# Products that nobody reads on TensorE ahead of six places where it waits, in a fused audio-tower kernel

## The reference

```python
h = _L0_tok_ref(x, ...)                       # merges 16 frames to 8 by a small softmax attention
h = h + _L0_attn_ref(_layernorm(h), ...)      # a Mamba block: input projection, causal convolution, scan, output projection
h = h + _L0_ffn_ref(_layernorm(h), ...)       # 8 experts, each token goes to its best two
h = h + _L1_attn_ref(_layernorm(h), ...)      # linear attention with decay: (q k^T / sqrt(d) * M) v
h = h + _L1_ffn_ref(_layernorm(h), ...)       # 3 experts, each sequence of 32 tokens goes to its best one
```

## Time and profile before

| | |
|---|---|
| median of 3 runs | 624.76 us (622.01 to 624.86) |
| the profiled execution, its own time | 630.95 us |
| its span, first to last instruction | 628.8 us |
| mean granted TensorE clock in the span | 0.899 |
| busy: PE / PEld / DVE / ACT / POOL | 520.4 / 452.6 / 359.6 / 242.8 / 222.8 us |

### The profile page before, as it was taken

One profiled execution on the slowest core, in us unless ns is written; L12 is line 12 of the kernel. 1 busy time (PEld: TensorE's weight loads), 2 busy tenths in 40 slices (PEclk: granted clock), 3 DMA queues, 4 the chain that ended last, 5 costly groups with the idle time before them and its releaser, 6 DMA issues. The chain is left out here.

```text
span 628.8 us, 11806 instructions
## 1 busy us (share of the span) xinstructions
PE 520.4 (83%) x3467; PEld 452.6 (72%) x3467; DVE 359.6 (57%) x1116; ACT 242.8 (39%) x579; POOL 222.8 (35%) x332
## 2 busy tenths in 40 slices
PE   4999879959989612999999999997687842999995
PEld 3667768847877502899999999995576741889994
DVE  2466538887999796444545454442456643445543
ACT  1368756664675250222222222222535541222230
POOL 1144500004977420212121221203777313466541
PEclk9999859988999755999999999997579985899998
DMA  9992000005232260131131311111335321122210
GB/s 263 244 205 50 2 0 2 0 2 145 83 104 71 73 276 7 39 95 39 53 87 47 92 45 45 40 37 40 88 88 158 99 78 33 49 65 63 64 52 19
DMA packets 39766, 47.84 MB, mean 76 GB/s; under 512 B 5633, under 2 KB 33618, under 8 KB 39586
## 3 DMA queue, kind: packets, MB, share of 16 engines
q1 hardware_dynamic: 32754, 33.48, 19.1%
q0 software_dynamic: 6000, 12.30, 7.2%
q10 hardware_dynamic: 960, 1.38, 0.8%
HBM read 31.56 MB, written 10.32 MB: 67 GB/s over the span
## 5 line engine op out<-in xcount | busy, mean ns | idle before, releaser
L1469 ACT ACTIVATE hidden_room<-psum 128x768 f32<-128x768 f32 x57 | 46.2, 811 | 206.6 <-PE psum L1429 193.7
L1380 POOL DMA_INDIRECT rows_in<-x,token x57 | 56.2, 986 | 176.3 <-PE psum L1407 155.3
L1513 DVE TENSOR_TENSOR rows_turned<-psum,rows_turned 128x128 fp32r<-128x128 f32 x57 | 16.6, 292 | 122.4 <-ACT rows_turned L1462 93.8
L1451 PE MATMUL psum<-w_proj,hidden_room 128*128 x468 | 82.6, 326 | 1.1 <-DVE hidden_room L1504 1.1
L1451 PEld LDWEIGHTS psum<-w_proj,hidden_room 128*128 128x128 f32 x468 | 75.1, 190 | 1.4 <-issue 1.3
L1429 PE MATMUL psum<-w_fc_high,rows_turned 128*128 x234 | 64.1, 356 | 8.1 <-DVE w_fc_low L1476 8.0
L1504 DVE COPY hidden_room<-psum 128x512 f32<-128x512 f32 x114 | 58.4, 552 | 3.5 <-PE psum L1438 0.9
L1438 PE MATMUL psum<-const,hidden_room 128*128 128x128 f32 x342 | 47.7, 276 | 0.9 <-ACT hidden_room L1469 0.9
L705 PE MATMUL psum<-w_fc_high 97*128 (+3 forms) x192 | 47.9, 413 | 0.6 <-PEq L401 0.6
L1429 PEld LDWEIGHTS psum<-w_fc_high,rows_turned 128*128 128x128 f32 x234 | 39.3, 192 | 12.3 <-issue 8.7
L788 DVE SCALAR_TENSOR_TENSOR conv_out<-psum,param,conv_out 128x496 f32<-128x496 f32 (+2 forms) x60 | 41.6, 715 | 8.0 <-ACT conv_out L727 6.6
(11 more groups left out here) (279 smaller groups left out, 1112.1 us busy)
## 6 DMA issues: line engine op xcount, KB each, us to landing
xbc_tile<-xbc SPq DMA_DIRECT2D x16, 320.0 KB, 2.8
w_proj<-in_w_proj SPq DMA_DIRECT2D x1, 4608.0 KB, 14.5
y<-rows_out SPq DMA_DIRECT2D x39, 96.0 KB, 1.6
sz<-in_x SPq DMA_DIRECT2D x16, 192.0 KB, 7.3
w_fc_low<-in_w_fc SPq DMA_DIRECT2D x2, 1536.0 KB, 30.8
w_fc_low<-in_w_fc SPq DMA_DIRECT2D x1, 2304.0 KB, 17.6
w<-in_w SPq DMA_DIRECT2D x3, 576.0 KB
x<-xf_tile SPq DMA_DIRECT2D x16, 96.0 KB, 1.6
```

Source lines behind the costliest of these rows:

```text
L1380: nc.gpsimd.indirect_dma_start(out=x[:, t.odd, 0:D], out_offset=None, in_=src, in_offset=bass.IndirectOffsetOnAxis(ap=tile_token[:, t.i:t. ...
L1451: last = nc.tensor.matmul(ps_y, ht[:, t.odd, ch, :], w_down[:, bass.ds((e * HC + ch) * D, D)], start=ch == 0, stop=ch == HC - 1)
L1469: act.activation(hid[:, t.odd, :], ps_h[t.odd], gelu).then_inc(act_done, 1)
L1513: nc.vector.tensor_tensor(xt[:, t.odd, REST, :], ps_x[:, 0, :], xt[:, t.odd, FIRST, :], ALU.subtract).then_inc(x_low, 1)
```

## The change

It adds a helper `stay_busy`, which issues a number of float32 products of a 128x128 tile with itself, and calls it at these places on PE: 9 products at the very start of the kernel (on a new tile that DVE sets to ones first), 6 ahead of the wait for the first frames, 4, 4 and 2 ahead of the first three `score`s; 28 after the last product of the projection; 7 when half and 7 when three quarters of the experts' low weights are ready, both ahead of `up(0)` of the first experts; 6 ahead of each of the first four `turn`s of the linear attention, after a new wait for `h3`; 4 after the last product of the sequence dispatch, 7 ahead of the loop over tiles of the second experts, and 3 ahead of their `up(0)`. That is 105 products. They write to a part of PSUM that nobody reads then; nothing waits for them but PE itself, whose queue is in order. Nothing is removed.

```diff
+def stay_busy(nc, to, of, count):
+
+    for _ in range(count):
+        nc.tensor.matmul(to, of, of, start=True, stop=True)
...
             @block.tensor
             def _(pe):
+                pe.wait_ge(square_set, 1)
+                stay_busy(nc, ps_none, square[:, :], 9)
                 pe.wait_ge(early, 16)
                 pe.wait_ge(w_ready, 3)
                 nc.tensor.transpose(ps_wv, wv_sel[:, :], c["ident"]).then_inc(wv_mm, 1)
 
                 def project(t):
+                    if t.i == 0:
+                        stay_busy(nc, ps_none, square[:, :], 6)
                     pe.wait_ge(x_in[t.i], 16)
...
                 def score(t):
+                    if t.i < 3:
+                        stay_busy(nc, ps_none, square[:, :], (4, 4, 2)[t.i])
                     pe.wait_ge(qk_ev, t.i + 1)
...
             @block.vector
             def _(dve):
+                nc.vector.memset(square[:, :], 1.0).then_inc(square_set, 1)
                 dve.wait_ge(early, 16)
...
                 with pe.Fori(1, N_TOK // SB) as j:
                     superblock(j)
+                pe.wait_ge(taps, 3 * (5 * (N_TOK // SB - 1) + 1))
+                stay_busy(nc, banks[0][:, 0:P], m.c["ident"], 28)
...
         nc.tensor.matmul(banks[3][:, 0:3 * T2], in_group[:, :], in_tile[:, :, :].rearrange("p w t -> p (w t)"), start=True, stop=True).then_inc(spread_mm, 1)
+        stay_busy(nc, banks[4][:, 0:P], m.c["ident"], 4)
...
         pe.wait_ge(routed.experts_set, 1)
+        if merge:
+            stay_busy(nc, ps_t[0][:, 0:P], c["ident"], 7)
...
         def up(t):
             if split and isinstance(t.i, int) and t.i == 0:
+                for done in (n_exp // 2, n_exp * 3 // 4):
+                    pe.wait_ge(split.low_ready, done)
+                    stay_busy(nc, ps_t[0][:, 0:P], c["ident"], 7)
                 pe.wait_ge(split.low_ready, n_exp)
             e = taken[t.i]
+            if merge and t.i == 0:
+                stay_busy(nc, ps_t[0][:, 0:P], c["ident"], 3)
             pe.wait_ge(x_out, x_outs * (t.i + 1))
...
                 def turn(t):
+                    if t.i < 4:
+                        pe.wait_ge(h3, t.i + 1)
+                        stay_busy(nc, ps[:, 7, 0:P], c["ident"], 6)
                     pe.wait_ge(std_set, t.i + 1)
```

More of the change, by code:

```diff
@@ L352, in merge_frames @@
         w_qk = sb("w_qk", [P, 2, G])
+        square = sb("square_that_nobody_reads", [P, P])
+        square_set = sem("square_set")
+        ps_none = banks[7][:, 0:P]
         wq_sc = sb("wq_scaled", [P, G])
```

## The result

The changed kernel takes 614.28 us (median of 4 runs, 613.46 to 617.17), the kernel before 624.81 us in the runs beside them (4 runs, 622.01 to 625.58). The ratio is 0.9845, with an interval of 0.9807 to 0.9883, so the kernel is faster by 1.2 to 1.9%. The ratios in this document leave out executions that lie over 1.5% above the fastest of their kernel, which is one reason why they differ from the quotients of the medians. The prediction was 609.0 us, in a range of 604.5 to 619.5: right in sign, inside the range, and right in the mechanism of four of its five terms, but 5.3 us too low. The profiled execution of the changed kernel took 614.48 us (span 612.3, mean clock 0.922); that of before had taken 630.95.

What follows compares the result with a forecast made beforehand. The prediction took PE to set the pace in frame merging, at either clock level. Its terms, 8.5 + 0.4 + 1.7 + 3.4 + 1.8 = 15.8 us, taken from the 624.76 us median gave 609.0 us, range 604.5 to 619.5.

Steps and rivals of the forecast that it cites:

- Frame merging: Stage at the kernel's start: 25 products raise PE's clock early, saving 8.5 us (6.4 to 10).
- The step sum of the prediction: Frame merging: estimated tile steps from the first `project` to tile 7's add up to 23.8 us, 9.5 us saved.
- once up it stays there with the merging's own work: Frame merging: after the rise, the stage's own products hold the upper level, as from 37.20 to 70.40 us before.
- The first rival: Frame merging stays at the lower level until its bias rows, only later places gain: 619.5 us, chance 0.12.
- Projection's end: 28 products there let the state space's first products run at the upper level: 0.4 us gained (-0.8 to 1.3).
- First experts: 14 products in PE's wait for the low weights make `up(0)` run at the upper level: 1.7 us (1.2 to 1.8).
- Linear attention: 24 products ahead of the first four `turn`s shorten the steps from tile 2 to 4: 3.4 us (2.0 to 4.1).
- Second experts: 14 products before and between `turn_rows(0)` and `up(0)` make `up(0)` faster: 1.8 us gained (1.2 to 2.0).
- The sum: All five stage terms together: 15.8 us, taking the profiled 630.95 us to 615.2.
- It lies 6.2 us above the median of the runs, and I carry that distance over: Whole kernel: the profiled execution's distance to the median is kept, so 624.76 - 15.8 = 609.0 us.
- the slower rival: Everywhere: the clock doesn't answer to the products, which are only queue, costing 8.1 us: 632.9 us, chance 0.06.
- the one of no change: The clock rises, but DVE, POOL and transfers hold the stages' starts: 623 us, chance 0.06.

Runs made afterwards that it cites:

- experiment 1: The kernel before, run and profiled once more with no edit: 624.01 us, ratio 0.9971 against the kernel before.
- experiment 2: The kernel before with only the 25 products of frame merging added: 617.20 us, ratio 0.9917.
- experiment 3: The kernel before with only the 28 products of the first and second experts (14 each) added: 620.56 us, ratio 0.9917.
- experiment 4: The kernel before with only the 24 products of the linear attention added: 629.85 us, ratio 1.0043.
- experiment 5: The changed kernel, run once more with no edit: 612.69 us, ratio 0.9835 against the kernel before.
- experiment 6: The changed kernel without the 28 products at the projection's end: 610.81 us, ratio 0.9815 against the kernel before.
- experiment 7: The kernel before with only frame merging's 25 products, each with weights of 64 columns instead of 128: 616.83 us, ratio 0.9897.
- experiment 8: The changed kernel without the projection's 28 products and with the linear attention's only ahead of `turn(1)` and `turn(2)`: 611.27 us, ratio 0.9808.
- experiment 9: The changed kernel without the 28 products at the projection's end, a second time on another chip: 610.93 us, ratio 0.9867.
- Experiment 10: The changed kernel, its 28 kept, plus 7 products at the state space's start and 4 after its first product (the bridge): 610.52 us, ratio 0.9840.
- experiment 11: The changed kernel without the projection's 28 products, but with 7 and 4 more at the state space's start: 610.64 us, ratio 0.9853.
- experiment 12: The changed kernel without the projection's 28 products and without the 4, 4 and 2 ahead of merging's first `score`s: 610.37 us, ratio 0.9846.

## Why the prediction was right, and where it was off

Stage lengths of the profiled executions, from the starts of PE's first products in each, in us (merging from the span's start to the projection's first product; projection to the state space's first; state space up to the pair dispatch's first; first experts from `up(0)` to the fold's first product; linear attention from there to `turn(4)`; second experts from the sequence dispatch's first product to the end). The numbers 1 to 12 are the experiments:

```
stage            before      1      2      3      4  after      5      6      7      8      9     10     11     12
merging           86.26  88.33  77.27  86.39  94.32  77.16  77.59  77.75  77.79  77.39  77.46  78.79  76.67  75.64
projection        55.13  55.12  55.11  55.12  55.12  55.75  56.08  55.18  55.14  55.30  55.09  55.76  56.82  55.26
state space       78.43  81.08  78.94  79.40  78.45  79.28  79.49  77.63  79.34  77.90  78.42  76.78  76.65  77.45
first experts    185.45 185.43 185.43 183.96 185.61 183.93 183.93 183.98 185.51 183.93 183.94 183.96 183.92 183.94
linear attention  32.32  28.45  30.72  28.57  26.38  29.17  27.54  26.99  31.44  30.37  27.42  27.41  27.00  27.28
second experts   109.21 105.79 105.77 103.97 105.72 104.78 104.50 104.33 105.88 104.06 103.96 104.77 104.34 104.56
```

**Frame merging, predicted 8.5 us (6.4 to 10).** Between the two profiles 9.1 us (86.26 to 77.16). The mechanism is as predicted up to the last `score`. The step sum of the prediction (23.8 us from tile 0 to tile 7) was close, 23.5 measured (7.12 to 30.64), which is 9.8 us saved. Some of it is lost behind the last `score`, where "once up it stays there with the merging's own work" did not hold: the level falls at 62.6, and from that `score` to the projection it takes 16.8 us where it took 16.3. The size depends on the execution of before that one compares with: 86.3 to 94.3 us in the four profiles without these products (mean 88.8), 75.6 to 78.8 in the ten with them (mean 77.4). By the means that is 11.4 us, and 7.5 to 18.7 between the extremes. The first rival (merging stays low, 619.5) is out: in none of the profiles with the first products was L428's work at 1.55 us. The 64 columns of L428, in which the prediction saw a possible cause of the low level, do not keep it low by themselves (experiment 7), and neither do waits of PE (experiment 4). What keeps the unaided merging low stays open.

**Projection's end, predicted +0.4 us (-0.8 to 1.3).** This is the term that failed: no gain shows. Between the two profiles projection and state space together took 1.5 us more (133.56 to 135.03), and experiment 6 suggests a loss of up to 1.9 us, of which the later barrier is the part that had been costed (0.6 us; the projection takes 55.8 to 56.1 us with the 28, 55.1 to 55.3 without them and without the bridge). The prediction's words "it may fall in the shorter gap too" name what happened: PE waits 1.68 us for DVE behind the barrier and 1.04 us for a transfer, and the level falls at 134.3 us. It is up again at 141.1, 8.2 us behind L888's start (8.4 in experiment 5), where experiments 6, 9 and 12 have 5.2 to 6.3 us. That the later fall makes the later rise is a reading of these rows; experiments 2 and 7, without the 28, have 7.8 and 10.7 us, so a part of it is again the draw of the execution. Experiment 10 shows in its one profile that the gap is the reason for the fall: with it filled the level stays. The ten profiles without the 28 and without the bridge are 132.7 to 136.2 us long from the projection to the pair dispatch, so the 135.0 and 135.6 us with the 28 lie inside what the kernel draws anyway. The prize is small in any case, since DVE's `w_out` and the first tile's transfer release the stage's first products at either level.

**First experts, predicted 1.7 us (1.2 to 1.8).** 1.5 us in all profiles that have the 14 products (185.4 to 183.9), with `up(0)` at 2.05 us instead of 3.56. The 3.58 and 1.77 us of the prediction are steps of the chain of the second expert stage.

**Linear attention, predicted 3.4 us (2.0 to 4.1).** 3.2 us between the two profiles; by means 2.9 us (30.3 for the five without, 27.4 for the eight with all 24). `turn(0)` is 1.2 us late, as costed, and this is covered: `turn(2)` stands 20.95 us behind the fold's first product (13.37 + 7.58), where it stood at 21.13 (12.17 + 8.96), so "it stays where it is" holds. The mis-sized part is the next step: `turn(3)` comes 4.66 us later and not 3.56 + 0.6, because POOL's root takes 2.21 us and ACT's deviation waits for it. Four of the eight profiles with all 24 products have this step (the changed kernel's, 5, 9 and 12); in the other four it is 3.57 or 3.65 us.

**Second experts, predicted 1.8 us (1.2 to 2.0).** 4.4 us between the two profiles, but only 0.9 to 1.9 us against the four others in the table without them (105.7 to 105.9, now 104.0 to 104.8). The profile of before was 3.4 us longer than these here, with no edit between them. The two chains of waits, first of before and then of experiment 1, show that 1.3 us of this are no matter of the clock but a later landing of the first gathered rows, ahead of `turn_rows(0)`:

```profile
526.62 3.98 DMA w_fc_low<-h,token
...
527.44 2.69 DMA w_fc_low<-h,token
```

The other 2.1 us lie behind `turn_rows(0)` (97.84 against 95.72 us to the end), where the clock rose 8.5 us after it in the one and 6.3 us in the other.

**The sum** was 15.8 us, and between the two profiled executions it is 16.5 (630.95 to 614.48). That it came out so close is partly luck: the projection's end was 1.9 us worse than its term and the second experts 2.6 us better, and these two nearly cancel. The step that made the forecast too low is the next one: "It lies 6.2 us above the median of the runs, and I carry that distance over". The sum without it, 615.2 us, is near what the changed kernel takes (614.28 and 612.69). The 6.2 us were not a constant offset of profiled executions. As far as other profiles of these stages without added products tell, they were an unfavourable draw in the second experts (3.4 us, 1.3 of them the landing above) and the linear attention (0.9 to 3.9 us), 4.3 to 7.3 us together. Merging was not the cause, since its 86.26 us are the shortest of the four unaided ones. The split stays an estimate, because no profiled execution of before lay at the median. The changed kernel's own profiled executions lay closer to its medians (614.48 against 614.28, and 613.55 against 612.69 in experiment 5). So a gain read from a draw that was some 6 us too long is too large for the median, which gained 10.5 us.

The slower rival (632.9) and the one of no change (623) are out by the total, and the slower one by L441's 0.88 us too. The slower rival's mechanism does hold where products outlast the gap that they stand in (experiment 12).

The Trainium skill ("TensorE: Matmul & The Clock Gate", "What's actually happening") says that the number of products at the lower level at a kernel's start differs from run to run. These profiles agree that it differs, with 34.3, 41.9, 33.6 and 53.6 us for the first rise of the unaided merging. It also says that the ramp is under 1% of a typical kernel's span; the measurement differs for this kernel, 11.4 us of merging alone by the means, 1.8% of 626 us.

## What to carry to other kernels

Fifteen dense products that nobody reads, in a wait at the kernel's start that is free anyway, are the main part of this gain: with ten more ahead of the first `score`s, which experiment 12 shows to be unnecessary, they brought 9.0 us by the medians of experiment 2 and 0.8% by its ratio. The kernel before spread over 617 to 656 us, the changed one and its variants (experiments 5, 6 and 8 to 12) over 608 to 617. Put such products where the wait is longer than they are. At a barrier they brought nothing that the totals show, even with the waits up to the real work filled too. Before a clock's gain is costed from one profile, take a second profile of the same kernel: stages whose length differs between the two are drawn, not given (by the clock, and here by a transfer too), and a distance to the median must not be carried over to a kernel that no longer draws.

## What the runs showed of the hardware

- PE was busy for 93% of 48.4 us, and within them for all of 11.38 us, and stayed at the lower level (experiment 4). In all ten profiles with fifteen dense products at the start the level rose within 4.0 to 7.1 us of the start (experiments 2, 5 to 12 and the changed kernel). What in merging's own stream keeps it low was not settled; weights of 64 columns alone do not, and neither do waits of PE.
- Once up, the level survived gaps of 0.73 and 0.66 us close together (experiment 12). It fell in the 7.0 us at the barrier (experiment 6), and in the changed kernel with waits of 1.68 and 1.04 us behind the barrier.
- A float32 product of 128x128 took 0.46 us at the lower level (3.19 / 7, at 231.87 us) and 0.23 at the upper one when 28 stood in a row (6.41 / 28).
- The same instruction on POOL, a root of 128 numbers, was counted with 0.57 to 2.21 us within one stage, and the deviation on ACT started only behind it.
- The first gathered rows of the second experts landed 3.98 us after their issue in one execution and 2.69 us in another, with no edit between them (the kernel before and experiment 1).
